# A wide cross-attention phase on one core: three PSUM banks for projections and one for the outputs, and another order within a slot

## The reference

```python
qh = heads_split(q @ Wq)          # q = layernorm(x), 256 -> 16 heads x 64
kh = heads_split(k @ Wk)          # k = v = ctx_1024
vh = heads_split(v @ Wv)
dots = jnp.einsum('bhid,bhjd->bhij', qh, kh) * scale
dots = jnp.where(mask[:, None, :, :], mask_value, dots)
attn = jax.nn.softmax(dots, axis=-1)
out = jnp.einsum('bhij,bhjd->bhid', attn, vh)
out = out.transpose(0, 2, 1, 3).reshape(b, n, h * d)
out = out @ Wo + bo               # added to x
```

## Time and profile before

| | |
|---|---|
| median of 3 runs | 2682.62 us (2681.57 to 2683.76) |
| profiled execution | 2668.03 us, its span 2666.1 us |
| PE busy over the span | 2234.8 us (84%), 23896 matmuls |
| DVE, ACT, POOL busy | 1565.4 (59%), 1366.1 (51%), 953.9 us (36%) |
| phase of the change, first scores to last output | 1336.9 to 1984 us of the span |

### The profile page before, as it was taken

How to read it: one execution, slowest core, us unless ns; L and a number is a source line. 1 busy time by engine, 2 the same in 40 slices (tenths; PEclk the granted TensorE clock), 3 DMA queues, 4 the chain that set the end, 5 groups by cost and what they waited for, 6 DMA issues and landing times. The chain is left out here.

```text
span 2666.1 us, 62362 instructions
## 1 busy us (share of the span) xinstructions
PE 2234.8 (84%) x23896; PEld 1471.6 (55%) x23896; DVE 1565.4 (59%) x3648; ACT 1366.1 (51%) x2903; POOL 953.9 (36%) x1066
## 2 busy tenths in 40 slices
PE   4898579689999999958589999999974993899846
PEld 2555345367777777636456656666652551566624
DVE  3666482476566565546766666666665644555465
ACT  2555463265555555425366666666653651455534
POOL 3443132154454444404422332332323742333125
PEclk8899689899999999969799999999986995899958
DMA  5553261310000000010200000000013214433034
GB/s 113 107 112 82 75 237 37 95 46 14 13 8 14 14 14 2 2 32 1 91 7 9 14 14 8 14 14 8 2 65 96 78 58 109 88 77 72 21 108 123
DMA packets 118579, 139.57 MB, mean 52 GB/s; under 512 B 15072, under 2 KB 107184, under 8 KB 118288
## 3 DMA queue, kind: packets, MB, share of 16 engines
q1 hardware_dynamic: 110900, 115.39, 16.7%
q0 software_dynamic: 7392, 20.19, 2.4%
HBM read 93.25 MB, written 17.47 MB: 42 GB/s over the span
## 5 line engine op out<-in xcount | busy, mean ns | idle before, releaser
L900 DVE TENSOR_REDUCE a_mx<-a_pair 112x2 f32<-112x750 f32 x256 | 234.5, 934 | 202.8 <-PE a_pair L969 202.7
L1210 POOL TENSOR_TENSOR a_kp<-a_kp 125x512 f16<-125x512 f32 x192 | 217.6, 1158 | 259.1 <-ACT a_kp L1301 259.1
L308 POOL TENSOR_SCALAR a_P<-a_P,a_inv 112x375 f32<-112x375 f32 x256 | 148.4, 593 | 450.3 <-DVE a_inv L435 450.3
L836 ACT ACTIVATE a_PT<-a_pair 125x672 f32<-125x672 f32 x256 | 186.4, 731 | 100.0 <-PE a_pair L981 98.3
L430 DVE CUSTOM_DVE_ANT_0 a_masked<-a_s,a_mask_add 112x375 f32<-112x375 f32 x256 | 130.0, 546 | 156.2 <-PE a_s L556 156.2
L346 ACT ACTIVATE a_P<-a_masked,a_least 112x375 f32<-112x375 f32 x256 | 153.5, 601 | 81.6 <-DVE a_least L430 81.6
L520 PE MATMUL a_p<-a_kc,a_wk 128*128 128x375 f16 x768 | 148.4, 330 | 21.0 <-DVE a_k L460 10.2
L534 PE MATMUL a_p<-a_wv,a_kc 128*125 128x512 f16 x576 | 145.2, 389 | 10.5 <-DVE a_k L460 10.3
L1344 DVE SCALAR_TENSOR_TENSOR a_k<-a_p,a_k 128x375 f16<-128x375 f32 x128 | 69.3, 547 | 138.9 <-ACT a_k L1257 138.8
L1301 ACT CAST a_kp<-a_kp 125x512 f16<-125x512 f32 x192 | 110.4, 617 | 76.3 <-DVE a_kp L1363 76.3
L1443 PE MATMUL a_p<-a_kc,a_wk 128*128 128x375 f16 x768 | 142.2, 326 | 5.4 <-POOL a_kc L1202 5.4
(11 more groups left out here) (420 smaller groups left out, 5253.9 us busy)
## 6 DMA issues: line engine op xcount, KB each, us to landing
a_kc<-in_ctxT SPq DMA_DIRECT2D x64, 375.0 KB, 3.2
a_k<-a_k_parts SPq DMA_DIRECT2D x192, 93.8 KB
w_stage<-in_L_ffn_W SPq DMA_DIRECT2D x32, 512.0 KB, 5.3
w_stage<-in_L_ffn_ew SPq DMA_DIRECT2D x16, 512.0 KB, 5.9
w_stage<-expert_rows SPq DMA_DIRECT2D x16, 448.0 KB, 7.0
a_v_in_sb<-in_ctx SPq DMA_DIRECT2D x16, 375.0 KB
a_q<-a_q_parts SPq DMA_DIRECT2D x48, 112.0 KB, 3.6
w_stage<-in_L_ffn_W SPq DMA_DIRECT2D x16, 256.0 KB, 3.9
```

What stands on the lines that cost most here:

```text
L308: pool.tensor_scalar(P[:, p % 4, r, :], P[:, p % 4, r, :], inv[:, p % 4, r:r + 1], 1.0, ALU.mult, ALU.mult).then_inc(P_done, 1)
L836: act.activation(PT[:, p % 4, :, :], pair_bank[slot["turned", p]][0:KP, :, 0:KT * S], ACT.Exp).then_inc(exp_done, 1)
L900: dve.tensor_reduce(mx[:, b % 2, 2 * pair:2 * pair + 2], pair_bank[slot["score", p]][0:S, :, 0:SK], AX.X, ALU.max).then_inc(max_done, 1)
L1210: pool.tensor_tensor(kp16[:, LO, j, hf, r, :, :].rearrange("p c m -> p (c m)"), kp[:, n % 4, :], kp16[:, HI, j, hf, r, :, :].rearrange("p ...
```

## The change

It does these things, all in `wide_attention_phase`:

- `p_bank` has three banks and `y_bank` one, where both had two. A projection now waits for the low part of the unit three before it. The first `weigh` of every half waits for the `low_y` of the half just before it.
- DVE makes the low parts of all units of slot s-1 right after `least_of(s)`; none is made in its own slot any more.
- PE makes the projections of a slot before its output products: scores, turn, projections, `weigh`.

The diff, without the replacements of `% 2` by `% PB` that repeat in `low`, `evacuate` and `score`:

```diff
     TURN, WEIGH = 2, 3
+    PB = 3
@@
-        y_bank = [m.bank("y0"), m.bank("y1")]
-        p_bank = [m.bank("p0"), m.bank("p1")]
+        y_bank = m.bank("y")
+        p_bank = [m.bank(f"p{i}") for i in range(PB)]
 
         def count(unit):
 
-            return number[unit] // 2 + 1
+            return number[unit] // PB + 1
@@
                     act.copy(yT16[:, b % 2, HI, 4 * hf:4 * hf + 4, :],
-                             y_bank[hf][:, 0:4 * S].rearrange("p (n s) -> p n s", s=S)).then_inc(y_hi, 1)
+                             y_bank[:, 0:4 * S].rearrange("p (n s) -> p n s", s=S)).then_inc(y_hi, 1)
@@
                 for s in range(FIRST, LAST + 2):
                     if 0 <= s < NPAIR:
                         least_of(s)
-                    for unit in units_at(s - 1)[-2:]:
+                    for unit in units_at(s - 1):
                         low(unit)
                     if 0 <= s - 1 < NPAIR:
                         invert(s - 1)
@@
                         low_y(p // NP, p % NP // 4)
-                    for unit in units_at(s)[:-2]:
-                        low(unit)
@@
                 def project(unit):
                     kind, b, c = unit
                     n = number[unit]
-                    out = p_bank[n % 2]
-                    if n >= 2:
-                        pe.wait_ge(emptied[n % 2], n // 2)
+                    out = p_bank[n % PB]
+                    if n >= PB:
+                        pe.wait_ge(emptied[n % PB], n // PB)
@@
                     if blk == 0:
                         last = ("v", b, (2, hf))
-                        pe.wait_ge(emptied[number[last] % 2], count(last))
-                        if b >= 1:
-                            pe.wait_ge(y_done, 2 * (b - 1) + hf + 1)
+                        pe.wait_ge(emptied[number[last] % PB], count(last))
+                        if b + hf >= 1:
+                            pe.wait_ge(y_done, 2 * b + hf)
@@
                     if 0 <= s - TURN < NPAIR:
                         turn(s - TURN)
+                    for unit in units_at(s):
+                        project(unit)
                     if 0 <= s - WEIGH < NPAIR:
                         weigh(s - WEIGH)
-                    for unit in units_at(s):
-                        project(unit)
```

More of the change, by code:

```diff
@@ L228, in wide_attention_phase @@
         projected = m.sem("projected")
-        emptied = [m.sem(f"emptied{i}") for i in range(2)]
+        emptied = [m.sem(f"emptied{i}") for i in range(PB)]
         k_hi, k_done, q_hi, q_done = (m.sem(n) for n in ("k_hi", "k_done", "q_hi", "q_done"))
@@ L352, in evacuate @@
                     act.wait_ge(projected, n + 1)
-                    src = p_bank[n % 2]
+                    src = p_bank[n % PB]
                     if kind == "k":
@@ L445, in low_y @@
                     dve.tensor_tensor(yT16[:, b % 2, LO, 4 * hf:4 * hf + 4, :],
-                                      y_bank[hf][:, 0:4 * S].rearrange("p (n s) -> p n s", s=S),
+                                      y_bank[:, 0:4 * S].rearrange("p (n s) -> p n s", s=S),
                                       yT16[:, b % 2, HI, 4 * hf:4 * hf + 4, :], ALU.subtract).then_inc(y_done, 1)
@@ L460, in low @@
                         dve.scalar_tensor_tensor(k16[:, LO, c, :], src[:, 0:SK], 1.0 / WS, k16[:, HI, c, :], ALU.mult,
-                                                 ALU.subtract).then_inc(emptied[n % 2], 1)
+                                                 ALU.subtract).then_inc(emptied[n % PB], 1)
                     elif kind == "q":
@@ L464, in low @@
                         dve.scalar_tensor_tensor(q16[:, b % 2, LO, c, :], src[:, 0:GW], -float(HD) ** -0.5 / WS,
-                                                 q16[:, b % 2, HI, c, :], ALU.mult, ALU.subtract).then_inc(emptied[n % 2], 1)
+                                                 q16[:, b % 2, HI, c, :], ALU.mult, ALU.subtract).then_inc(emptied[n % PB], 1)
                     elif kind == "v":
@@ L475, in low @@
                         dve.scalar_tensor_tensor(X[:, b, :], src[0:S, 0:D], 1.0 / WS, X[:, b, :], ALU.mult,
-                                                 ALU.add).then_inc(emptied[n % 2], 1)
+                                                 ALU.add).then_inc(emptied[n % PB], 1)
                 dve.wait_ge(w_hi, 1)
@@ L503, in _ @@
                             low_x(g)
-                for i in range(2):
-                    dve.wait_ge(emptied[i], (len(order) + 1 - i) // 2)
+                for i in range(PB):
+                    dve.wait_ge(emptied[i], len(range(i, len(order), PB)))
             @block.tensor
@@ L548, in score @@
                     g, t = divmod(b, GT)
-                    pe.wait_ge(emptied[number["k", b, c] % 2], count(("k", b, c)))
+                    pe.wait_ge(emptied[number["k", b, c] % PB], count(("k", b, c)))
                     if t == 0:
-                        pe.wait_ge(emptied[number["q", g, c] % 2], count(("q", g, c)))
+                        pe.wait_ge(emptied[number["q", g, c] % PB], count(("q", g, c)))
                     if p >= 1:
@@ L581, in weigh @@
                             for r in range(2):
-                                mm = pe.matmul(y_bank[hf][64 * r:64 * r + HD, blk * S:(blk + 1) * S],
+                                mm = pe.matmul(y_bank[64 * r:64 * r + HD, blk * S:(blk + 1) * S],
                                                v16[0:KP, b % 2, j, z, (2 * c + r) * HD:(2 * c + r + 1) * HD],
```

## The result

The changed kernel takes 2707.98 us, the median of 4 runs (2703.53 to 2712.55), against 2682.1 before (2681.24 to 2683.76, 4 runs): 25.9 us slower, ratio 1.0092 with a 95% interval of 1.0078 to 1.0105. I had said 2720, slower, with a range of 2697 to 2743.

What follows compares the result with a forecast made beforehand. PE's list bounds the phase (busy 606 of 647 us). Output waits +40.6, less gains from banks, start and mode, gave +22; clock falls +16.5 made +38.7, so 2720 us, range 2697 to 2743.

Steps and rivals of the forecast that it cites:

- The wait for the outputs: Slots with s mod 8 of 3 or 7: with one y bank, weigh needs the same slot's low_y; together +40.6 us.
- The offset 4.95: Slots mod 3 behind a q slot: low_y released 4.95 us behind the scores, so the slot lasts 5.52 against 3.48.
- the sign that I had given: In slots mod 7, weigh would be released by DVE's low_y, as in slots mod 3.
- Pauses of 0.26: Slots mod 0, 2 and 5: the pause before the first projection goes with the third bank, 45 x 0.26 = -11.7 us.
- slots mod 6: With q, lost pauses offset by v's wait for the output projection's bank: nothing; without q, +0.44 each, +1.3 us.
- PE's mode: Turn beside projections: three half/whole-array changes per slot, not four; 0.09 each in 75 slots, bounds 0 to -7, taken -3 us.
- The start: Slot 6: v's bank is free, -3.0 us; slots before 6 some shorter pauses, -2; slots 38 and 70 nothing.
- The clock: PE's clock falls behind 11 of the 15 waits in slots mod 3, 1.5 us each: +16.5, bounds 0 to +25.
- the first rival: The waits come but PE's clock stays: 2705 us, 2697 with all bounds at their low ends; chance 0.22.
- The sum: All terms: +22 us without the clock, +38.7 with it; 2668.0 to 2706.7 profiled, 2720 as the median.
- The rival without any fall: The output waits come and PE's clock never falls: 2682.6 + 22 = 2705 us; chance 0.22.

Runs made afterwards that it cites:

- e1: The changed kernel run again with no edit: 2693.2 us, ratio 1.0091 to the kernel before.
- e3: Changed kernel with take_y first in its slot on ACT and low_y behind the first low part on DVE, one y bank kept: 2662.85 us, ratio 0.9978.
- e4: Changed kernel with outputs emptied early and the first of three low parts back in its own slot: 2630.64 us, ratio 0.985 to before.
- e5: Kernel before with only PE's order changed, projections ahead of output products, two banks and two: 2716.01 us, ratio 1.0179.
- e6: Changed kernel with PE's order undone, output products ahead of projections, three banks and one kept: 2802.72 us, ratio 1.0514 to before.
- e7: e4 with the inverse of pair s-1 put ahead of least_of(s) on DVE: 2623.23 us, ratio 0.9825 to the kernel before.
- e2: Changed kernel with the low part of the first of three units made in its own slot again: 2677.31 us, ratio 1.003 to before.

## Why the prediction was right, and where it was not

**The wait for the outputs: right.** I had +40.6; by the slots it is 12 x 2.0 + 3 x 1.79 + 12 x 0.84 - 3 x 0.26 and 1.8 in slot 127, together 40.5. That it came so close is luck in part: the 1.8 of slot 127 holds a slow clock, and e1, without it there, has 0.8. The offset 4.95 came out as 4.90 (the output products of slot 51 start 1607.96 - 1603.06 behind the scores). What made it work was to read off the timeline of before when `low_y` ends, though nobody waited for it then. e3 shows the cause by taking the wait away, and it shows its share too. Slots mod 3 and 7 lose 27.5 us by it, 0.6 of them falls of the clock. Another 14.4 us stay in these slots behind a q, 9.2 of them in mod 7, where the prediction had put 0.2 of its 0.88 down to the wait and the rest to the place of the projections: in the changed kernel these output products come so soon behind v's end (0.06) that no wait on a_yT is listed for them, against the sign that I had given. What held them was the low parts, as e4 shows, in which mod 7 goes from 5.40 to 4.28.

**Pauses of 0.26: right, slots mod 6 and PE's mode undersized.** Slots mod 0, 2 and 5 lost their pause. They lost 0.10 to 0.14 more, and mod 4 lost 0.10, because the turn takes 0.74 with a projection behind it (1598.26 to 1599.00) and took 0.84 with output products. I had bounded this at 0 to 7 us and taken 3. (The kernel before does have one turn with a projection right behind it, in slot 2, but that projection waits 0.82 for DVE, so the price could not be read there.) In the 60 slots mod 0, 2, 4 and 5 it is 7.5, of which the turn's 0.10 in each makes 6; what the rest in mod 2 and 5 comes from was not looked for. By the Trainium skill (TensorEngine Tiling (Array Packing), Key Properties) a change of mode drains the engine. The trace agrees in the direction, and the whole -7 was nearer than my -3. e5, with the old banks, has the shorter turn as well (mod 1 and 4 at 4.28 for 4.38), and e6, with the old order, the 0.84 again. That the switch of mode is what costs is a reading of these: the runs show that the cost depends on what follows the turn. PE's busy time in the phase fell by 7.8 us, where I had said that it would grow only by the slow stretches. In slots mod 6 behind a q, which I had at nothing, 0.18 went in each, 1.7 us in nine of them.

**The start: right.** Slots 0 to 5 gave 1.8 (I had 2), slot 6 gave 3.3 (I had 3.0). Slot 38 gave 1.8 that I had at nothing, as the clock did not fall there this time.

**A term that was missing: slots mod 1.** Slots mod 1 last 4.55 where 4.38, less 0.10 for the turn, was to be had, so they lost 0.26 and are 0.16 longer than before, 2.5 us in 15 slots. I had looked at this chain for the low parts and not for the softmax that POOL scales. e7 shows the cause for most of it, in that an earlier inverse takes 0.18 of the 0.26 away. I take the shorter slot mod 0 before it for the reason that the softmax is now late; that was not tried by itself. It fits it that in e5, with slot mod 0 at 3.90, the slots mod 1 last 4.28 and lose nothing, while in e2 and e4, with slot mod 0 at 2.98 and the low parts in their old places, they still last 4.54.

**The clock: the step that failed.** "I take 11 x 1.5 = +16.5." The price of one fall was right, the number was not: the changed kernel had 3 falls behind its 15 slots mod 3, in the same places in both of its profiles. Slot 107 in the timeline, its k, its output products behind a wait of 2.08, the scores and the turn of slot 108:

```profile
1893.91 1.13 PE L519 MATMUL a_p<-a_kc,a_wk 128*128 128x375 f16 x6
1897.12 1.05 PE L581 MATMUL a_y<-a_PT,a_v 125*64 125x112 f16 x18 [2.08 <-DVE a_yT L446]
1898.10 1.19 PE L555 MATMUL a_s<-a_k,a_q 64*112 64x375 f16 x6
1899.21 1.53 PE L565 MATMUL a_t<-all_ident,a_P 112*125 112x112 f32 x6
```

And the granted clock around it (0.65 over these 3 us):

```profile
1896.20:1899.20 3.00, 2.08 (x24) 1.34 (x24) 0.77 (x2) 0.44 (x2) 0.49 (x1) 0.65 0.00 0
```

From start to start, output products took 0.98 for 0.57, scores 1.11 for 0.62, turn 1.37 for 0.75: 1.5 us for one fall. Three falls cost 4.7 us, against 16.5. Of the 12 slots with two waits (0.75 and 1.50, a k between) one had a fall, of the 3 with one wait of 2.08 two. I had counted both kinds alike, with two waits close together as bad as a long one; in these rows they are not. The Trainium skill (TensorE: Matmul & The Clock Gate, HAM oscillation) blames longer gaps, as I wrote at the first rival. That did not hold either: e2 shows falls behind 8 waits of 2.08. What decides between two equal waits stays open.

**The sum.** Without the clock I had +22.2, and it is 20.8 less 4.7, so 16.1: slots mod 0, 2, 4 and 5 with their modes (-4.5), slots mod 6 (-1.8), the start with slots 38 and 70 (-2.2) and slots mod 1 (+2.5) are the difference. With the clock I had +38.7 and it is 20.8 in the phase, 25.9 and 23.8 in the two comparisons of medians. So the 2720 was 12 too high. The rival without any fall, 2705, was nearer, by luck: it had none of the 4.7 of the clock, but its +22.2 was 6 too high, and the two nearly cancel. The direction and the mechanism were as forecast. The lengths of slots came within 0.07 in mod 3 and 7, and within 0.18 elsewhere.

## What to carry to other kernels

When two buffers become one, find in the trace when the contents of the remaining one leave, measured from the start of the same step, and compare that with when its next user comes: the price can be read before any run, though nobody waits yet. A scarce buffer can be given away at no cost if the engines that empty it do so first in their step (here two moved calls turned +24 us into -7, and with the first of three low parts back in its own slot, into -39). An order of PE and the placing of its banks have to be tried together: the order alone cost 46 us, the rest of the change without it 132.

## What the runs showed of the hardware that I had not expected

The fall of PE's clock is not decided by the length of the wait alone: the same wait of 2.08 us, in the same place of a repeating order, had a fall behind 8 slots and none behind 7 (e2). Two profiled executions of the changed kernel have their falls at the same three slots mod 3, but not the same clock behind slot 127. Waits of 3.04 to 3.39 had one in 29 of 30 slots (e6, slots 7 to 123), and in e3 and e4, where the waits of slots mod 3 are 0.75 and 0.55, none. A turn with a full-array product behind it took 0.74 to the next start, and 0.84 with a half-array product, in every slot that no wait or slow clock touched.
